# A two-layer decoder on one core: the clearings between GpSimd's indirect DMAs become a quarter as wide

## Chip, core and metric

The kernel runs on one core of one Trainium2 chip. The metric is the device time of one execution in microseconds. Engines are named as in the profile: PE is TensorE (PEld its weight loads), DVE is VectorE, ACT is ScalarE, POOL is GpSimd, SP is SyncE, which here only issues DMAs.

## What is computed

4,096 tokens of width 128 (x is 64 x 64 x 128, float32) pass six blocks. Each adds its result to its input and normalises over the 128 columns:

```python
x = _layernorm(x + _L0_attn_ref(x, ...))              # retention with xpos, group norm and gate
x = _layernorm(x + _L0_xattn_ref(ctx_2048, x, mask, mask, ...))   # masked cross-attention
x = _layernorm(x + _L0_ffn_ref(x, ...))               # 8 experts, the top 2 after rerouting by similarity
x = _layernorm(x + _L1_attn_ref(x, ...))              # 16 heads, values outside a band set to 0
x = _layernorm(x + _L1_xattn_ref(x, ctx_2048, ...))   # context joined to keys and values
x = _layernorm(x + _L1_ffn_ref(x, ...))               # encoder layer with a top-2 mixture of 8 experts
```

Two of these need rows to be moved by an index that is known only on the chip. In the third block every token picks two of its eight expert results. In the sixth every token's row goes to two experts, and two results come back.

## The kernel before

The tokens are cut into 16 groups of 256 (T = 2 tiles of 128). A group has number n * 4 + s: s is one of four slots, each with its own buffers in SBUF and two PSUM banks, and n counts four passes. The stages are:

1. First layer (about the first 477 us of the span). All eight expert results of a group are stored to a tensor y_mid of its own in HBM, and the state to x_mid.
2. Second layer (about 477 to 1375 us). For every group GpSimd fetches the two chosen expert rows of each token from y_mid by indirect DMA (`fetch`, stage "ya", L1038), and VectorE adds them up (L1583). Then come attention, cross-attention and the sixth block's own attention. At its end (stage "sc", L1102) GpSimd scatters each token's row by indirect DMA to two places in rows_x, ordered by expert.
3. Experts (1375 to about 1540 us). 39 tiles of 256 rows are loaded from rows_x, go through the expert's two matrices, and are scattered to y_rows (L1112).
4. The results are added, normalised and stored.

Every engine has one queue, and its order is written out by hand (`ORDERS`): a list of pairs (group, so many stages). `in_turn` walks through it, so instructions of four to six groups alternate on each engine, and an engine never goes past one that waits. Between engines semaphores pass (`x.of(s)`, `x.at(n, s)`). `root` (L972, L973) is the short piece of every layer norm that GpSimd does: variance plus epsilon, then the power -0.5. VectorE applies the result (L1387) and TensorE turns the normalised rows (L1829).

A fetch and a scatter are four indirect DMAs each, one for every tile t of 128 tokens and every choice k. Between two of them stands `clear_again`, three times in a fetch and three times in a scatter; the last two scatters (pass 3, slots 2 and 3) have none. It sets `blank` to zero again and, through `pool2`, makes GpSimd wait for its own instruction. `blank` is a tile of 128 x 528 float32 (4 * WIDE, where WIDE = 132 is the width of a row of rows_x). It is cleared at the start (L955) and then read by four DMAs of SyncE that fill rows_x with zeros (L844). GpSimd waits for these before the first fetch. After that nothing reads `blank`.

Other lines that the rows name: L1277, L1272 and L1625 move queries and keys out of PSUM, L1688 and L1319 spread keys and queries of the sixth block's attention, L1691 and L1630 add the bias to its values, L1065 and L1066 set parts of V and Q for the cross-attention (stage "out1"), L1059 scales attention weights.

Of the kernel before, what the change touches and what calls it, by code (L numbers as in the profile page):

```python
# [46 lines left out]
WIDE = DIM + 4  # L47
# [407 lines left out]
def build(nc, d, out, groups):  # L455
    passes = groups // SLOTS
    ctx = ExitStack()
    with ctx:
        def sb(name, shape, dt=F32):
            return ctx.enter_context(nc.sbuf_tensor(name, shape, dt))  # L460

        def sem(name):
            return ctx.enter_context(nc.semaphore(name))
# [58 lines left out]
        blank = sb("blank", [128, 4 * WIDE])  # L522
# [240 lines left out]
        dve2, pool2 = Steps(sem("dve2")), Steps(sem("pool2"))  # L763
# [190 lines left out]
        def _(pool):  # L954
# [71 lines left out]
                return pool.tensor_tensor(X1[s][:, :, :], X1[s][:, :, :], over(Row(b), T), ALU.add)  # L1026

            def clear_again():
                pool2(pool, pool.memset(blank[:, :], 0.0))

            def fetch(n, s):
                if n == 0 and s == 0:
                    pool.wait_ge(s_clear, 16 * (XROWS // 128 // BLANK))
                for t in range(T):
                    for k in range(2):
                        if t or k:
                            clear_again()
                        pool.indirect_dma_start(y_two[s][:, k, 128 * t:128 * t + 128], None, d[f"y_mid{n * SLOTS + s}"][:, :], bass.IndirectOffsetOnAxis(  # L1038
                            ap=first_rows[:, (n * SLOTS + s) * T + t, k:k + 1], axis=0)).then_inc(y_loaded[s], 16)
# [35 lines left out]
            def second2(n, s, last):  # L1075
                yield "fq.1"
                with_bias(n, s, b_x, b_x_bias, "fbo", 2)
                pool.wait_ge(b_x_ps.of(s), b_x_ps.at(n, s, use=2))
                pool.wait_ge(b_x_bias.of(s), b_x_bias.at(n, s, use=2))
                pool.tensor_tensor(X[s][:, :, :], X[s][:, :, :], over(Row("be2"), T), ALU.add).then_inc(b_x_be2.of(s), 1)  # L1080
                pool.wait_ge(b_frot.of(s), b_frot.at(n, s, 2))
                pool.tensor_tensor(qf[s], P4[s][:, 0, :], P4[s][:, 1, :], ALU.add).then_inc(b_fsum.of(s), 1)
                yield "fq.3"
                pool.wait_ge(b_frot.of(s), b_frot.at(n, s, 4))
                pool.tensor_tensor(kf[s], P4[s][:, 2, :], P4[s][:, 3, :], ALU.add).then_inc(b_fsum.of(s), 1)
                if not last:
                    yield "ya"
                    pool.wait_ge(b_s_ps.of(s), b_s_ps.at(n, s, use=5))
                    fetch(n + 1, s)
                yield "fo"  # L1090
                root(n, s, b_ln_mv, b_ln_rstd, pool2, 3)
                yield "n3"
                pool.wait_ge(b_ln_x1.of(s), b_ln_x1.at(n, s, use=0))
                scale_shift(s, "g1", "be1").then_inc(b_x1.of(s), 1)
                yield "sc"
                pool.wait_ge(b_g_done.of(s), b_g_done.at(n, s))
                pool.wait_ge(b_x1.of(s), b_x1.at(n, s))
                for t in range(T):
                    for k in range(2):
                        if (t or k) and (n < passes - 1 or s < SLOTS - 2):  # L1100
                            clear_again()
                        pool.indirect_dma_start(d["rows_x"][:, :], bass.IndirectOffsetOnAxis(  # L1102
                            ap=places[:, (n * SLOTS + s) * T + t, k:k + 1], axis=0), XW[s][:, t, :], None).then_inc(scattered[s], 16)
# [1227 lines left out]
```

## Time and profile before

| | |
|---|---|
| median of 3 runs | 1593.64 us |
| lowest and highest | 1590.29 and 1594.18 us |
| span of the profiled execution (the one time shown of it) | 1609.1 us |
| TensorE busy | 1400.8 us, 87% |
| VectorE busy | 1118.0 us, 69% |
| ScalarE busy | 933.2 us, 58% |
| GpSimd busy | 710.2 us, 44% |
| mean granted clock of TensorE | 0.953 of full speed |

The span is one execution under the profiler; the runs are timed without it. Durations and places in time below are all from that execution, in us from its start. Busy is the time in which an engine ran an instruction; issuing a plain DMA and waiting do not count. "Idle before" of an instruction is what its engine waited just before it, and the name behind the arrow is who released it.

### The profile page before, as it was taken

What the parts mean: (1) busy time and instruction counts of PE and PEld (TensorE: products, weight loads), DVE (VectorE), ACT (ScalarE), POOL (GpSimd) and SP (SyncE); (2) the same over time, 40 slices, a digit from 0 to 9 for tenths busy, and PEclk for the clock granted to TensorE, in tenths of its full rate; (3) what the DMA queues carried; (4) which work ended last, traced back from release to release, by engine and by line L of the source; (5) the groups of instructions that cost most, each with busy time, mean ns of one, the idle gap of its engine ahead of it and who ended that gap; (6) DMA issues with size and microseconds to landing.
All of it is one profiled execution on the core that took longest, in us unless ns stands there. A gap on an engine that the chain in (4) does not pass through costs nothing.

```text
span 1609.1 us, 47442 instructions
## 1 busy us (share of the span) xinstructions
PE 1400.8 (87%) x19262; PEld 1135.4 (71%) x19262; DVE 1118.0 (69%) x3476; ACT 933.2 (58%) x2469; POOL 710.2 (44%) x1048
## 2 busy tenths in 40 slices
PE   6899999999987998889989899987999985699961
PEld 4688788788765777667767677765677764588851
DVE  3777777877866657788667787677885866445456
ACT  3455556655633587754878556885568863344412
POOL 5514434434216215565244754256651343345455
PEclk8799999999998999999999999999999987799985
DMA  9942212111121001110001100011010001577761
GB/s 329 384 152 77 63 64 80 57 54 64 38 81 38 9 9 29 33 30 29 9 17 29 38 25 20 12 32 32 25 29 6 19 20 66 171 229 235 213 176 40
DMA packets 112155, 123.21 MB, mean 77 GB/s; under 512 B 21984, under 2 KB 85216, under 8 KB 111680
## 3 DMA queue, kind: packets, MB, share of 16 engines
q1 hardware_dynamic: 105344, 106.53, 21.0%
q0 software_dynamic: 6592, 13.64, 2.6%
q8 instruction: 152, 2.49, 0.7%
q14 instruction: 67, 0.55, 0.1%
HBM read 64.99 MB, written 55.15 MB: 75 GB/s over the span
## 4 chain that ended last, share of the span: by engine, by line
PE 54%; DVE 21%; ACT 9%; POOL 8%; issue 6%; another core or an unknown queue 1%; DMA 1%; SPq 0%; DVEq 0%; POOLq 0%; ACTq 0%
PE bank L1970 6%; PE bank L1837 5%; PE bank L2217 4%; PE bank L2224 4%; ACT P L1247 3%; PE bank L2092 3%; PE bank L1822 3%; PE bank L2057 3%; PE bank L1849 3%; POOL rows_x L1102 2%; PE bank L2018 2%; PE bank L2014 2%; PE bank L2007 2%; DVE P L1602 2%; PE bank L1937 2%
## 5 line engine op out<-in xcount | busy, mean ns | idle before, releaser
L1837 PE MATMUL bank<-const,P 128*128 128x128 f32 x1152 | 174.1, 283 | 14.5 <-ACT P L1247 6.1
L1837 PEld LDWEIGHTS bank<-const,P 128*128 128x128 f32 x1152 | 132.0, 144 | 48.8 <-ACT P L1247 15.5
L1247 ACT ACTIVATE P<-bank,gs 128x128 f32<-128x128 f32 x512 | 142.3, 392 | 32.2 <-DVE gs L1591 30.8
L1970 PE MATMUL bank<-XT,wb 128*128 128x256 f32 x512 | 143.2, 401 | 7.7 <-ACT PT L1152 4.3
L1059 POOL TENSOR_TENSOR P<-P,gs 128x512 f32<-128x512 f32 x64 | 66.6, 1048 | 152.5 <-DVE gs L1638 152.0
L1255 ACT ACTIVATE PT<-bank 128x512 f32<-128x512 f32 x192 | 110.5, 614 | 35.6 <-PE bank L1837 34.7
L1601 DVE TENSOR_REDUCE gs<-bank 128x8 f32<-128x512 f32 x128 | 87.3, 682 | 40.8 <-PE bank L1822 23.5
L1112 POOL DMA_INDIRECT y_rows<-R,gidx x78 | 74.7, 957 | 92.3 <-DVE R L1777 78.6
L1591 DVE TENSOR_REDUCE gs<-bank 128x4 f32<-128x512 f32 x128 | 83.0, 684 | 43.6 <-PE bank L2092 43.4
L1970 PEld LDWEIGHTS bank<-XT,wb 128*128 128x128 f32 x512 | 88.6, 193 | 25.0 <-ACT PT L1152 8.6
L972 POOL TENSOR_SCALAR rstd<-mv 128x2 f32<-128x2 f32 x80 | 17.9, 224 | 195.1 <-DVE mv L1379 194.2
L1348 ACT ACTIVATE PT<-bank,Q 128x256 f32<-128x256 f32 x156 | 64.6, 475 | 56.7 <-PE bank L2217 49.3
L1240 ACT ACTIVATE P<-P 128x512 f32<-128x512 f32 x128 | 81.5, 644 | 24.2 <-DVE P L1602 22.1
L1219 ACT ACTIVATE P<-bank 128x256 f32<-128x256 f32 x128 | 48.5, 380 | 77.6 <-PE bank L1970 76.9
L1602 DVE TENSOR_TENSOR P<-bank,gs 128x512 f32<-128x512 f32 x128 | 88.5, 692 | 4.4
L2217 PE MATMUL bank<-XT,Q 128*128 128x256 f32 x312 | 86.1, 388 | 2.9 <-ACT XT L1344 2.7
L2224 PEld LDWEIGHTS bank<-Q,PT 128*128 128x128 f32 x624 | 79.5, 192 | 7.0 <-issue 3.3
L1102 POOL DMA_INDIRECT rows_x<-XW,places x64 | 64.4, 1006 | 44.8 <-DVE places L1728 28.9
L1849 PE MATMUL bank<-wb,P 128*128 128x128 f32 x512 | 79.5, 280 | 4.5 <-DVE P L1532 4.2
L2224 PE MATMUL bank<-Q,PT 128*128 128x128 f32 x624 | 81.2, 276 | 1.9 <-issue 1.8
L1849 PEld LDWEIGHTS bank<-wb,P 128*128 128x128 f32 x512 | 72.5, 192 | 14.1 <-DVE P L1532 9.7
L1038 POOL DMA_INDIRECT Q<-y_mid,first_rows x64 | 63.4, 990 | 31.8 <-DVE first_rows L1577 16.1
(298 smaller groups left out, 3815.0 us busy)
## 6 DMA issues: line engine op xcount, KB each, us to landing
Q<-in_wm SPq DMA_DIRECT2D x39, 578.5 KB
rows_x<-blank SPq DMA_DIRECT2D x4, 5016.0 KB, 37.8
y_mid<-PT SPq DMA_DIRECT2D x16, 512.0 KB, 2.9
y_mid<-D SPq DMA_DIRECT2D x16, 512.0 KB, 2.9
XW<-rows_x SPq DMA_DIRECT2D x39, 132.0 KB
wb<-in_wb SPq DMA_DIRECT2D x1, 4228.0 KB, 15.5
V<-in_ctxT SPq DMA_DIRECT2D x32, 128.0 KB, 2.7
XT<-in_xT SPq DMA_DIRECT2D x16, 128.0 KB, 2.2
```

The lines of the kernel that those rows point to most:

```text
L1102: pool.indirect_dma_start(d["rows_x"][:, :], bass.IndirectOffsetOnAxis(ap=places[:, (n * SLOTS + s) * T + t, k:k + 1], axis=0), XW[s][:, t ...
L1240: act.activation(P[s][:, i, :], P[s][:, i, :], ACT.Exp, scale=scale).then_inc(p.of(s), 1)
L1247: ins = act.activation(P[s][:, i, 128 * g:128 * g + 128], banks[s][i][:, 128 * g:128 * g + 128], ACT.Exp, bias=gs[s][:, 0, 4 * i + g:4 * i ...
L1255: act.activation(dst[:, i, :], banks[s][i][:, :], ACT.Copy).then_inc(pT.of(s), 1)
L1591: dve.tensor_reduce(gs[s][:, 0, 4 * i:4 * i + 4], banks[s][i][:, :].rearrange("p (g m) -> p g m", m=128), AX.X, ALU.min).then_inc(b_s_sub. ...
L1601: st2(dve.tensor_reduce(mx, v, AX.X, most))
L1602: dve.tensor_tensor(P[s][:, i, :].rearrange("p (g m) -> p g m", m=width), v, each(mx, width), ALU.subtract).then_inc(s_sub.of(s), 1)
L1837: last = pe.transpose(tile(banks[s][i], t), tile(P[s][:, i, :], t), ident)
L1849: last = mm(tile(half(s, i + 1), t), tile(P4[s][:, i + 1, :], t), tile(B("down"), e), start=True, stop=True)
L1970: mm(half(s, 2 * (e % 2) + k), tile(B("gu"), 2 * e + k), XT[s][:, :], start=True, stop=True).then_inc(a_up_ps.of(s), 1)
L2217: mm(half(s, c), tile(part(wm[s], WM, "w1"), c), XT[s][:, :], start=True, stop=True).then_inc(m_up_ps.of(s), 1)
L2224: ins = mm(tile(half(s, 0), t), tile(PT4[s][:, c, :], t), tile(part(wm[s], WM, "w2"), c), start=c == 0, stop=c == NC - 1)
```

## The change

The 90 later clearings write columns 0 to 131 of `blank` and not all 528. The first clearing, which the DMAs read, stays as wide as it was.

```diff
             def clear_again():
-                pool2(pool, pool.memset(blank[:, :], 0.0))
+                pool2(pool, pool.memset(blank[:, 0:WIDE], 0.0))
```

## Rows read from the trace of the kernel before

**Rows 1.** The page's head: busy us, share of the span, instructions.
```profile
span 1609.1 us, 47442 instructions
PE 1400.8 (87%) x19262; PEld 1135.4 (71%) x19262; DVE 1118.0 (69%) x3476; ACT 933.2 (58%) x2469; POOL 710.2 (44%) x1048
```

**Rows 2.** The page: the chain that ended last, by engine.
```profile
PE 54%; DVE 21%; ACT 9%; POOL 8%; issue 6%; another core or an unknown queue 1%; DMA 1%; SPq 0%; DVEq 0%; POOLq 0%; ACTq 0%
```

**Rows 3.** Groups of GpSimd: shapes, count, busy us, mean ns, idle before.
```profile
L1029 POOL MEMSET blank<- 128x528 f32 x90 | 50.0, 555 | 0.2
...
L1066 POOL MEMSET V<- 128x256 f32 x16 | 5.0, 311 | 0.0
...
L964 POOL MEMSET Q<- 128x16 f32 x4 | 0.3, 125 | 0.1
```

**Rows 4.** Timeline of GpSimd in one scatter: start, us, instruction, idle before.
```profile
667.18 1.09 POOL L1102 DMA_INDIRECT rows_x<-XW,places  x1 [0.43 <-DVE places L1728]
668.28 0.56 POOL L1029 MEMSET blank<- 128x528 f32 x1
669.12 1.00 POOL L1102 DMA_INDIRECT rows_x<-XW,places  x1 [0.28 <-POOL blank L1029]
670.11 0.56 POOL L1029 MEMSET blank<- 128x528 f32 x1
670.95 0.97 POOL L1102 DMA_INDIRECT rows_x<-XW,places  x1 [0.28 <-POOL blank L1029]
```

**Rows 5.** The chain in order of time: first and last of 33 clearings.
```profile
477.55 0.57 POOL blank L1029
...
1311.08 0.55 POOL blank L1029
```

**Rows 6.** Timeline of GpSimd in the last two scatters.
```profile
1364.39 0.96 POOL L1102 DMA_INDIRECT rows_x<-XW,places  x1 [0.30 <-issue]
1365.66 0.96 POOL L1102 DMA_INDIRECT rows_x<-XW,places  x1 [0.31 <-issue]
```

**Rows 7.** Timeline of TensorE where the chain returns from GpSimd, directly or not.
```profile
491.26 0.69 PE L1829 MATMUL bank<-const,X 128*128 128x128 f32 x2 [7.94 <-DVE X L1387]
...
502.73 0.46 PE L2030 MATMUL bank<-K,Q 64*64 64x64 f32 x16 [0.57 <-DVE V L1630]
...
679.84 1.10 PE L1822 MATMUL bank<-D,Q 64*64 64x128 f32 x32 [1.61 <-DVE V L1691]
...
700.90 0.44 PE L1829 MATMUL bank<-const,X 128*128 128x128 f32 x2 [1.63 <-DVE X L1387]
...
740.19 0.44 PE L1829 MATMUL bank<-const,X 128*128 128x128 f32 x2 [0.44 <-DVE X L1387]
...
893.06 1.81 PE L1822 MATMUL bank<-D,Q 64*64 64x128 f32 x32 [1.46 <-ACT Q L1319]
...
952.17 0.44 PE L1829 MATMUL bank<-const,X 128*128 128x128 f32 x2 [0.17 <-DVE X L1387]
...
972.53 0.44 PE L1829 MATMUL bank<-const,X 128*128 128x128 f32 x2 [1.21 <-DVE X L1387]
...
1164.29 0.66 PE L1837 MATMUL bank<-const,P 128*128 128x128 f32 x4 [1.09 <-POOL P L1059]
...
1314.64 0.69 PE L1829 MATMUL bank<-const,X 128*128 128x128 f32 x2 [0.76 <-DVE X L1387]
```

**Rows 8.** Timeline of other engines at those places.
```profile
677.76 1.60 DVE L1688 TENSOR_SCALAR D<-K,const 128x256 f32<-128x256 f32 x2 [0.64 <-POOL K L1085]
...
698.84 0.60 DVE L1387 TENSOR_SCALAR X<-R,mv,rstd 128x128 f32<-128x128 f32 x2 [1.28 <-POOL rstd L973]
...
891.25 1.70 ACT L1319 ACTIVATE Q<-K,const 128x256 f32<-128x256 f32 x4 [0.81 <-POOL K L1082]
...
970.90 1.56 DVE L1387 TENSOR_SCALAR X<-R,mv,rstd 128x128 f32<-128x128 f32 x2 [0.42 <-POOL rstd L973]
...
1308.31 0.97 POOL L1102 DMA_INDIRECT rows_x<-XW,places  x1 [1.50 <-issue]
```

**Rows 9.** Stretches: us, busy us and count by engine, granted clock, DMA share, GB/s.
```profile
684.00:691.00 7.00, 7.00 (x154) 6.24 (x152) 5.79 (x29) 3.66 (x9) 3.19 (x4) 0.68 0.12 32
1313.00:1320.00 7.00, 6.03 (x31) 4.83 (x31) 2.87 (x8) 1.15 (x3) 5.36 (x9) 0.51 0.08 23
```

## The prediction

> **What bounds the kernel now.** I read the page's head first, then the chain of work that ended last, then GpSimd's groups, and last the timeline around each clearing that stands on the chain. The head shows TensorE busy in 87% of the span and GpSimd in 44% [rows 1]. The chain gives TensorE 54% of the span, VectorE 21%, ScalarE 9% and GpSimd 8% [rows 2]. The kernel is therefore bound by TensorE and by the hand-overs to it, and GpSimd matters only where its queue is the last thing that others wait for. That happens around the indirect DMAs: GpSimd runs its stages in a fixed order, so the small root (L972, L973) that a layer norm waits for stands behind four indirect DMAs and three clearings.
>
> The groups show 90 clearings of 128x528 at 555 ns, 50.0 us together [rows 3]. The timeline of one scatter shows the beat: indirect DMA 1.09, clearing 0.56, 0.28 of hand-over, next DMA [rows 4]. I then went through the chain in eighteen stretches of 90 us and counted: 33 of the 90 clearings are on it, the first at 477.55 and the last at 1311.08 [rows 5]. The other 57 lie beside longer work.
>
> **The change part by part.** Only the width of the memset changes. No instruction, DMA, wait or place in a queue is added, removed or moved. blank is read only by the four DMAs at the start, and nothing reads what the later clearings write.
>
> What a 128x132 memset takes is not in the trace, so I bound it. A 128x16 memset takes 125 ns and a 128x256 one 311 ns [rows 3]; these are the ends. Between them the slope is 186/240 = 0.775 ns a column, which gives 125 + 116 x 0.775 = 215 ns. Between 256 and 528 columns the slope is 244/272 = 0.90, which gives 311 - 124 x 0.90 = 200 ns. I take 208. A clearing then gives back 555 - 208 = 347 ns (244 to 430 at the ends). Ninety of them free 31.2 us of GpSimd. A group of three, which is one fetch or one scatter, gives 1.04 us. The 33 on the chain give 33 x 0.347 = 11.5 us at most.
>
> Could the indirect DMA refuse to come sooner, so that a wait replaces the clearing? In the last scatters, which have no clearings, the next one starts 0.30 us after the end of the one before and still takes 0.96 us [rows 6]: a beat of 1.26 us. The new beat would be 0.96 + 0.21 + 0.28 = 1.45 us, slower than that, so nothing of the kind stands in the way.
>
> How much of the 11.5 us arrives? GpSimd comes earlier by up to 1.04 us a group; an engine can use of that only what it had been idle just before, since its own queue is late next. The ten places where a stretch of the chain with clearings returns to the others [rows 7, 8]:
>
> - 491.26, behind two fetches (six clearings): TensorE had been idle 7.94 us. All of 6 x 0.347 = 2.08 counts.
> - 502.73, behind the third fetch: idle 0.57. 0.57.
> - 679.84, behind a scatter: TensorE idle 1.61, but VectorE's D (L1688), which hands over to it, had been idle only 0.64. 0.64.
> - 700.90: idle 1.63. 1.04.
> - 740.19: idle 0.44. 0.44.
> - 893.06: TensorE idle 1.46, but it waits for ScalarE's Q (L1319), and that one had been idle 0.81. 0.81.
> - 952.17: idle 0.17. 0.17.
> - 972.53: TensorE idle 1.21, but VectorE's X (L1387) only 0.42. 0.42.
> - 1164.29: idle 1.09. 1.04.
> - 1314.64: idle 0.76. One of the three clearings there is followed by 1.50 us in which GpSimd waited for nothing shown [rows 8]; I take it that this gap stays and swallows its share, and count two: 0.69.
>
> The sum is 7.90 us, 69% of 11.5. That is after one meeting with other queues. Behind each place come further ones, where another slot's work is late next. I have no row that adds these up; I take the same share once more, 7.90 x 0.69 = 5.4 us. The 57 clearings off the chain I cost at nothing. Their cover is TensorE's work of other slots, and the relief only keeps their groups from becoming late when the rest moves up by 5 us. If the cover went, they would be worth at most 57 x 0.347 = 19.8 us, which I see no sign of: TensorE's idle time outside those ten places is spread over other releasers.
>
> The port between VectorE and GpSimd: VectorE's pair of normalisations (L1387) takes 0.60 us at 698.84, and 1.56 us at 970.90, where GpSimd runs memsets of V and Q alongside (the stage "out1", L1065 and L1066) [rows 8]. So a memset of GpSimd can hold up a VectorE operation of this form. The Trainium skill, page SBUF — State Buffer, section "Who interferes with whom", states that VectorE in a two-port mode and GpSimd exclude each other for a whole instruction; by it this pair is what rows 8 show, and shorter clearings would hold VectorE for less. The rule has a side that speaks against the change as well: an indirect DMA that comes sooner takes the port sooner. Out of rows, GpSimd's instructions fill (0.96 + 0.56)/1.79 = 85% of a beat before and (0.96 + 0.21)/1.45 = 81% after, so the balance is slightly in favour, and I cost it at nothing.
>
> The sum is made on the profiled execution (span 1609.1 us, the one time of it that is shown); the median of the runs is 15.5 us below. A difference of 5.4 us carries over: 1593.6 - 5.4 = 1588.2 us, -0.34%.
>
> **The rivals.**
>
> *A. Hidden (no change).* GpSimd's relief is taken up by the other queues a few microseconds later. For: TensorE is busy 87% of the span, and at three returns (740.19, 952.17, 972.53) an idle time of 0.44 us or less caps the gain [rows 7, 8]. Against: the opening at 491.26 is a plain stall of 7.94 us with nothing else to do, and it alone gives 2.1 us. If only that and a third of the remaining 5.8 us arrive, the time is 1593.6 - 4.0 = 1589.6; if only that, 1591.6. Both are within 0.3% (4.8 us), which is about what a measurement of this kernel can tell from no change.
>
> *B. All of it, and clock on top.* Every clearing on the chain pays, 11.5 us: 1582.1. Right behind two of the returns TensorE's granted clock is down: 0.68 over 684 to 691 and 0.51 over 1313 to 1320, that is at 1.2 instead of 2.4 GHz for two thirds or nearly all of the time, each after idle time of TensorE [rows 9]. If a smaller stall there no longer brings the clock down, 6.03 us of matmuls at 0.51 become 6.03 x 0.51 = 3.1 us, another 2.9 us each. One such stretch beside 7.9 us of relief gives 1582.8.
>
> *C. Slower: the clock the other way.* The same mechanism with the opposite sign. Places where TensorE now keeps 2.4 GHz see its idle time fall elsewhere when GpSimd's hand-overs come earlier than the partner's, and gain low stretches. One stretch like that of 1313 to 1320 costs 2.9 us. It decides the sign from the second (5.8 against 5.4 us), and four net (11.6 - 5.4 = +6.2, 1599.8) make it slower by over 0.3%. For: low stretches come after stalls of 1 to 2 us, and there are many places near that. Against: order and work of every engine stay as they were, every release comes no later than before, and idle time of TensorE shrinks on the whole.
>
> *D. The change does not do what it says,* because a memset has a floor near the old price: excluded by the 125 and 311 ns rows [rows 3].
>
> **How the numbers follow.** The forecast (4.8 to 9 us less) gets 0.45, B (9 us or more less) 0.09, A (within 4.8 us of before) 0.40, C 0.06. So faster by over 0.3% is 0.54, within 0.3% 0.40, slower by over 0.3% 0.06. The predicted time is 1588.2. Downwards the range ends at 1581.5, just past the full 11.5 us; upwards at 1594.5, which takes in A whole and a low stretch of the clock that eats the 2.1 us of the opening.
>
> **What would show it right or wrong.** In the profile of the changed kernel: L1029 still 90 times, near 208 ns; GpSimd's busy time down by 31 us to 679; the beat inside a fetch at 1.45 us with the indirect DMAs still at 0.95 to 0.97; the stall at 491.26 down from 7.94 to about 5.9 us; the ten returns earlier by the amounts above, within their caps. TensorE's busy time should stay within the few microseconds that its clock moves. The prediction is wrong if the indirect DMAs grow longer when they follow each other sooner, if the 0.28 us of hand-over grows by what the clearing lost, or if low stretches of the clock come or go in number: that is the largest term I cannot size, some 3 us each.

## The result and the profile after

The changed kernel takes 1572.22 us (median of 4 runs, 1568.92 to 1576.02); the kernel before took 1593.91 us in the same session (1590.29 to 1598.14). The ratio is 0.9868 with a 95% interval of 0.9843 to 0.9894: 21 us or 1.3% faster, between 17 and 25 us. The forecast was 1588.2 us, 5.4 us faster, with a range down to 1581.5. The sign was right and the size was a quarter of the real one.

The profiled execution of before that the prediction rests on was a long one: 1609.1 us of span [rows 1], while the run of the second profile below took 1594.15 us for a span of 1592.3. The kernel before was therefore profiled once more (experiment 1). Where not said otherwise, "before" is now that second profile. The head of the page and the chain by engine, first of before, second profile:

```profile
span 1592.3 us, 47442 instructions
PE 1394.5 (88%) x19262; PEld 1133.8 (71%) x19262; DVE 1117.1 (70%) x3476; ACT 935.3 (59%) x2469; POOL 710.2 (45%) x1048
...
PE 52%; DVE 22%; POOL 10%; ACT 9%; issue 6%; DMA 1%; SPq 0%; DVEq 0%; POOLq 0%; ACTq 0%
```

and of the changed kernel:

```profile
span 1569.1 us, 47442 instructions
PE 1385.0 (88%) x19262; PEld 1124.8 (72%) x19262; DVE 1114.3 (71%) x3476; ACT 934.2 (60%) x2469; POOL 680.4 (43%) x1048
...
PE 54%; DVE 21%; ACT 9%; POOL 8%; issue 5%; DMA 1%; SPq 0%; DVEq 0%; POOLq 0%; ACTq 0%
```

GpSimd is busy 29.8 us less. TensorE, with the same 19,262 matmuls, is busy 9.5 us less (15.8 less than in the first profile of before, whose 1400.8 us show how far two executions differ); the forecast put that at nothing. The groups of GpSimd in the changed kernel:

```profile
L1102 POOL DMA_INDIRECT rows_x<-XW,places x64 | 64.4, 1006 | 44.5 <-DVE places L1728 29.4 <-POOL blank L1029 11.4 <-issue 3.7
L1038 POOL DMA_INDIRECT Q<-y_mid,first_rows x64 | 63.4, 990 | 31.8 <-DVE first_rows L1577 16.1 <-POOL blank L1029 13.0 <-issue 2.7
...
L1029 POOL MEMSET blank<- 128x132 f32 x90 | 20.3, 226 | 0.2
```

A clearing takes 226 ns and not 555 [rows 3], so each gives back 329 ns and all ninety 29.7 us. The indirect DMAs take what they took. The same scatter as in [rows 4], in the changed kernel:

```profile
659.31 1.09 POOL L1102 DMA_INDIRECT rows_x<-XW,places  x1 [0.43 <-DVE places L1728]
660.41 0.23 POOL L1029 MEMSET blank<- 128x132 f32 x1
660.92 0.97 POOL L1102 DMA_INDIRECT rows_x<-XW,places  x1 [0.28 <-POOL blank L1029]
661.88 0.23 POOL L1029 MEMSET blank<- 128x132 f32 x1
662.39 0.97 POOL L1102 DMA_INDIRECT rows_x<-XW,places  x1 [0.28 <-POOL blank L1029]
```

The beat is 1.47 us and was 1.8; the hand-over of 0.28 us is untouched.

**Where the time went.** The first indirect DMA starts at 473.0 us in both traces, so the first layer gave nothing. From the last scatter's last DMA to the end it is 1592.3 - 1361.5 = 230.8 us and 1569.1 - 1339.1 = 230.0. All but 0.8 us of the difference lies between, in the second layer. I cut it at the first DMA of the scatters number 1, 4, 5, 8, 9 and 12, which gives three stretches with scatters and two long pieces between them. A stretch holds three scatters and two fetches, 15 clearings; the long piece behind it holds the fourth scatter and two fetches, 9 clearings, with some 80 us without any between them. The columns are us, busy us and count of TensorE, its weight loads, VectorE, ScalarE and GpSimd, then TensorE's granted clock. Before:

```profile
662.25:747.53 85.28, 74.31 (x1158) 57.77 (x1159) 69.68 (x217) 45.00 (x113) 53.27 (x72) 0.94 0.10 30
747.53:877.28 129.75, 121.80 (x2191) 94.29 (x2189) 92.04 (x226) 102.13 (x278) 52.50 (x80) 0.99 0.08 21
877.28:956.51 79.23, 71.15 (x1155) 55.50 (x1156) 66.89 (x216) 44.53 (x111) 53.52 (x72) 0.98 0.11 32
956.51:1086.58 130.07, 119.61 (x2190) 92.71 (x2190) 92.67 (x225) 101.68 (x277) 52.47 (x81) 1.00 0.08 21
1086.58:1169.44 82.86, 72.76 (x1153) 56.76 (x1151) 66.70 (x214) 43.83 (x109) 52.99 (x72) 0.96 0.11 31
```

Changed:

```profile
659.31:738.01 78.70, 70.42 (x1158) 54.30 (x1159) 69.40 (x217) 44.67 (x113) 48.30 (x73) 1.00 0.11 33
738.01:867.97 129.96, 121.12 (x2191) 94.07 (x2189) 92.00 (x226) 101.98 (x277) 49.52 (x80) 0.99 0.08 21
867.97:944.38 76.41, 69.47 (x1157) 53.96 (x1156) 67.03 (x216) 44.56 (x112) 48.54 (x72) 1.00 0.11 34
944.38:1072.38 128.00, 119.68 (x2190) 92.73 (x2190) 91.47 (x225) 101.67 (x277) 49.72 (x80) 1.00 0.08 21
1072.38:1149.53 77.15, 70.15 (x1153) 53.66 (x1151) 65.88 (x214) 43.62 (x109) 48.03 (x72) 1.00 0.11 33
```

Up to the first scatter the changed kernel gains 662.25 - 659.31 = 2.9 us, all of it at the opening. The three stretches with scatters gain 6.6, 2.8 and 5.7 us, the two long pieces -0.2 and 2.1, and the rest, from scatter 12 to the last one's last DMA, 2.5 (192.1 and 189.6 us). The 15 clearings of a stretch are 4.9 us of relief, so two of the three gain more than their clearings give back. TensorE's busy time falls in them by 3.9, 1.7 and 2.6 us, and its granted clock rises from 0.94, 0.98 and 0.96 to 1.00.

How finely may one pair of profiles be read? The first indirect DMA, with the same work before it, starts between 473.0 and 477.6 us in the profiles of experiments 1 to 9 and 12; that two of them agree at 473.0 is luck. Four profiles have the clearings of before: its own two and those of experiments 10 and 11. In them the three stretches take 83.6 to 85.3, 79.2 to 80.8 and 79.8 to 84.0 us, so a single stretch differs by up to 4 us from one execution to the next. The means of the four lie 5.8, 3.4 and 4.7 us above the changed kernel, 13.9 us together for 14.8 us of relief. The clock does go with the clearings: of the twelve stretches only one, in experiment 10, has it at 1.00, and all three do in the changed kernel. That one:

```profile
1086.58:1166.34 79.76, 70.16 (x1152) 53.62 (x1151) 66.54 (x214) 43.73 (x109) 53.04 (x72) 1.00 0.11 32
```

### The profile page after: what moved, and what is told of

It is laid out like the page before. It is cut to its first block, busy times and chain, and to the rows that moved or that the text cites. A ratio compares the mean times of both kernels' runs of the same rounds, so it can differ in the third digit from the quotient of the medians.

```text
span 1569.1 us, 47442 instructions
## 1 busy us (share of the span) xinstructions
PE 1385.0 (88%) x19262; PEld 1124.8 (72%) x19262; DVE 1114.3 (71%) x3476; ACT 934.2 (60%) x2469; POOL 680.4 (43%) x1048
## 4 chain that ended last, share of the span: by engine, by line
PE 54%; DVE 21%; ACT 9%; POOL 8%; issue 5%; DMA 1%; SPq 0%; DVEq 0%; POOLq 0%; ACTq 0%
PE bank L1970 6%; PE bank L1837 5%; PE bank L2217 4%; PE bank L2224 4%; ACT P L1247 3%; PE bank L2057 3%; PE bank L2092 3%; PE bank L1849 3%; PE bank L2018 3%; POOL rows_x L1102 2%; PE bank L2007 2%; PE bank L1822 2%; PE bank L2014 2%; DVE P L1602 2%; DVE gs L1601 2%
## 5 line engine op out<-in xcount | busy, mean ns | idle before, releaser
L1240 ACT ACTIVATE P<-P 128x512 f32<-128x512 f32 x128 | 82.1, 647 | 24.9 <-DVE P L1602 24.3
L1038 POOL DMA_INDIRECT Q<-y_mid,first_rows x64 | 63.4, 990 | 31.8 <-DVE first_rows L1577 16.1
## 6 DMA issues: line engine op xcount, KB each, us to landing
wb<-in_wb SPq DMA_DIRECT2D x1, 4228.0 KB, 15.1
```

The source lines that it names most:

```text
L1240: act.activation(P[s][:, i, :], P[s][:, i, :], ACT.Exp, scale=scale).then_inc(p.of(s), 1)
```

## The experiments

Each kernel was timed in five rounds beside the kernel before; times in us are medians, intervals belong to the ratio.

**1. The kernel before again.** No edit.

> The kernel before, once more, for a second profile. The profiled execution of before had a span of 1609.1 us, 15 us above the runs, while that of the changed kernel (1569.1) lies 2 us below its runs. Theory N (the first profile was a slow draw, its extra low stretches of TensorE's clock are not the kernel's own): the span here is 1588 to 1598 and the low stretches between 477 and 1337 us add up to under 40 us. Theory K (the low stretches are tied to the stalls behind the indirect DMAs, at every execution): the same seven low stretches in that part, about 44 us. Time in both: same as before, ratio 1.00.

Measured: 1594.15 against 1593.53 (1.0007, 0.9989 to 1.0024), span 1592.3. Theory N is right that the first profile had been a long draw, and wrong about the clock: between 477 and 1337 us the two profiles have 44.4 and 44.6 us at the lower level, as theory K said, though not at the same places. The chain, counted in pieces of 40 us, holds 45 of the 90 clearings here and not 33: the nine of the opening again, and 12 scatters where the first profile had 8. The four scatters that are new begin at 899, 1087, 1108 and 1169 us. No fetch behind the opening is on either chain. The first clearing on the chain, one of each new scatter, and the last:

```profile
474.24 0.57 POOL blank L1029
...
899.89 0.57 POOL blank L1029
...
1087.68 0.56 POOL blank L1029
...
1108.71 0.57 POOL blank L1029
...
1170.53 0.57 POOL blank L1029
...
1303.52 0.55 POOL blank L1029
```

**2. No clearings.**

```diff
-                pool2(pool, pool.memset(blank[:, :], 0.0))
+                pass
```

> No clearing at all between the indirect DMAs, so the beat falls from 1.79 to about 1.26 us (against 1.45 with 132 columns). The clearings after the first are left out; nothing reads them. Theory P (GpSimd's time is worth nearly a constant share wherever it is taken away: 21.7 us for 29.7 us of clearing, 0.73): GpSimd gets back 90 x 0.53 = 48 us, and the time falls by about 35 us, to 1559. Theory Q (the gain of 132 columns came from a shorter hold on the port that VectorE shares, so that removing the beat's free 0.28 us works the other way): the time is at or above that of the changed kernel, 1572 or more. Theory R (by the caps of the prediction, the gain runs out): about 1568, little below the changed kernel.

Measured: 1569.76 (0.9844, 0.9830 to 0.9857), 24.9 us faster. From 132 columns to none GpSimd gets back 18 us more and the time falls by about 4 us, less than the two intervals can tell apart. The gain runs out, as theory R had it, and theory P's 35 us is refuted. Theory Q (no faster than the changed kernel) is not: the difference is too small for that, and experiment 9 has to decide.

**3 and 4. Only the fetches, only the scatters narrow** (`clear_again` gets a width, WIDE in one of its two calls).

> 132 columns only in the 48 clearings of the fetches, 528 in the 42 of the scatters. Theory P: 48/90 of the gain, 11.6 us, ratio 0.993. Theory S (only the scatters count, since seven of the ten places on the chain are behind scatters; the fetches give the opening stall alone): 2 to 3 us, ratio 0.998.

> 132 columns only in the 42 clearings of the scatters. Theory P: 42/90 of the gain, 10.1 us, ratio 0.994. Theory S: 18 to 19 us, ratio 0.988. If both halves together with e3 make clearly less than 21.7 us, the two kinds cover for each other; if more, each alone already frees what the other would.

Measured: fetches 1589.07 (0.9969, 0.9958 to 0.9981), 4.9 us for 15.8 us of relief; scatters 1579.19 (0.9909, 0.9894 to 0.9924), 14.5 us for 13.8 us of relief. Together 19.4, near the whole. The expectation of equal shares is refuted by both. Theory S had 2 to 3 us for the fetches, the near edge of what was measured (3.0 to 6.7), and 18 to 19 for the scatters, above what was measured (12 to 17). A scatter's clearings are worth about all of their time. A fetch's are worth a third on average, but the nine of the opening alone give 3 us, as the timeline further down shows, so that the 39 others are left with some 2 us for 12.8 us of relief.

**5. Two short clearings for one.**

```diff
-                pool2(pool, pool.memset(blank[:, :], 0.0))
+                pool2(pool, pool.memset(blank[:, 0:24], 0.0))
+                pool2(pool, pool.memset(blank[:, 0:24], 0.0))
```

> Each clearing becomes two of 128x24, each waited for: about 2 x (0.13 + 0.28) = 0.82 us between indirect DMAs, nearly the 0.83 of the kernel before, but GpSimd's memsets fill only 0.27 us of it and not 0.56. Theory P (GpSimd's time in its queue is what counts): as before, ratio 0.998 to 1.002. Theory Q (the hold on the port that VectorE shares is what counts): most of the 21 us gain comes, ratio 0.990 or less. In between: the share that the port has.

Measured: 1577.51 (0.9899, 0.9878 to 0.9921). The expectation had a wrong term: the second memset follows the first after 0.07 us, not 0.28, so the gap between DMAs (from the end of one to the start of the next) was 0.60 us and not 0.82. The kernel does not separate the theories; it is one more point on the line of gaps. In its trace:

```profile
661.89 1.09 POOL L1103 DMA_INDIRECT rows_x<-XW,places  x1 [0.43 <-DVE places L1729]
662.99 0.14 POOL L1029 MEMSET blank<- 128x24 f32 x1
663.19 0.12 POOL L1030 MEMSET blank<- 128x24 f32 x1
663.59 1.06 POOL L1103 DMA_INDIRECT rows_x<-XW,places  x1 [0.28 <-POOL blank L1030]
```

**6. Every clearing twice** (the memset of 528 columns stands there two times).

> Each clearing of 128x528 is made twice: 50 us more of GpSimd's time, beat 2.6 us or so with its second hand-over. Theory P (nearly every clearing lies on the path through the stretches with scatters, 0.65 us of time per us of GpSimd): at least 0.83 x 90 x 0.65 = 48 us slower. Theory R (caps: only the places on the chain, as the prediction had it, 33 to 45 of 90): 0.83 x 33 to 0.83 x 45 = 27 to 37 us slower.

Measured: 1645.26 (1.0323, 1.0300 to 1.0345), 51.5 us slower; gap 1.44 us, so 55 us more of GpSimd's time. Upwards 0.94 of every microsecond arrives. Theory R, by which only the clearings of the two chains count, is refuted: it allowed 37 us. Of the caps this run says nothing, since idle time before an instruction limits what it can gain and not what it can lose. In its trace:

```profile
672.75 0.56 POOL L1029 MEMSET blank<- 128x528 f32 x1
673.36 0.54 POOL L1030 MEMSET blank<- 128x528 f32 x1
674.18 0.98 POOL L1103 DMA_INDIRECT rows_x<-XW,places  x1 [0.28 <-POOL blank L1030]
```

**7 and 8. Narrow only where the first profile's chain had clearings (33), and only elsewhere (57).** A counter picks the groups:

```diff
+            NARROW = {"fetch": (0, 1, 2), "sc": (0, 1, 2, 4, 6, 7, 10, 12)}
...
+                width = WIDE if kinds[kind] in NARROW[kind] else 4 * WIDE
+                pool2(pool, pool.memset(blank[:, 0:width], 0.0))
```

> 132 columns only in the 33 clearings that the chain of the first profile holds (the first three fetches; the scatters number 1, 2, 3, 5, 7, 8, 11 and 13 in the order of the queue), 528 in the other 57. The prediction's bookkeeping: these alone carry the gain, 5.4 to 7.9 us, and the other 57 nothing, so this kernel would be as fast as the whole change. Theory P (the rest of the groups are late by next to nothing and count as well): 33/90 of 21.7 = 8 us here, and the remaining 13 to 14 us in the other kernel.

> The complement: 132 columns only in the 57 clearings that the chain of the first profile does not hold. The prediction's bookkeeping: 0 us, ratio 1.000. Theory P: 57/90 of 21.7 = 13 to 14 us faster, ratio 0.991. If the two kernels together give much less than 21.7 us, the gain needs both, because each group's relief is swallowed where the next group is still long.

Measured: on the chain 1580.46 (0.9920, 0.9902 to 0.9938), 12.8 us (10 to 16) for 10.9 us of relief; off it 1588.23 (0.9967, 0.9955 to 0.9979), 5.3 us (3 to 7) for 18.8 us. Together 18, not clearly less than 21. So the clearings on the first chain carry their relief fully (1.2 us a us), not at 0.47, and the rest is not free (0.28).

That the first chain picked the right clearings does not follow. Its 33 are the nine of the opening and 24 of scatters; the other 57 are 39 of fetches and 18 of scatters. By experiment 4 a scatter's clearing is worth 14.5 / 42 = 0.345 us. If each has that worth, on the chain or off it, the first kernel gains 3.0 + 24 x 0.345 = 11.2 us, which is inside what was measured, and the second 18 x 0.345 = 6.2, with about 2 us for the fetches 8. If a scatter off the first chain is worth nothing, the second has those 2 us alone. The measured 5.3 lies between. The chain of the second profile comes nearest: it adds four of the six scatters, 12 x 0.329 = 3.9 us, and with the fetches that makes 6. The runs do not separate the three.

**9. Time without memory.** One clearing of 24 columns and twelve empty instructions.

```diff
-                pool2(pool, pool.memset(blank[:, :], 0.0))
+                pool2(pool, pool.memset(blank[:, 0:24], 0.0))
+                for _ in range(12):
+                    apart(pool)
```

> Between indirect DMAs one clearing of 128x24 and twelve empty instructions, which touch no memory, in place of the clearing of 128x528. What the empty ones take isn't known; the trace gives the gap g from the end of one indirect DMA to the start of the next. The kernels so far give for gaps of 1.44, 0.83, 0.60, 0.50 and 0.30 us the times +51, 0, -16.8, -21.4 and -24.8 us. Theory P (only time in GpSimd's queue counts): the time at this gap lies on that line. Theory Q (what counts is the hold on VectorE's port): at a gap near 0.83 the time is still 10 us or more under the line, since GpSimd's memsets fill 0.13 us of the gap and not 0.56.

Measured: 1601.98 (1.0051, 1.0035 to 1.0068), 8.1 us slower. Its trace:

```profile
668.48 0.14 POOL L1029 MEMSET blank<- 128x24 f32 x1
669.41 0.99 POOL L1104 DMA_INDIRECT rows_x<-XW,places  x1 [0.79 <-POOL blank L1029]
670.39 0.14 POOL L1029 MEMSET blank<- 128x24 f32 x1
671.31 0.96 POOL L1104 DMA_INDIRECT rows_x<-XW,places  x1 [0.78 <-POOL blank L1029]
```

The gap is 0.92 us, 0.09 more than before; 90 x 0.09 = 8.1 us, and the line through gaps 0.83 and 1.44 gives 0.09 x 51.5/0.61 = 7.6 us. The memset fills 0.14 us of the gap and not 0.56, and nothing of a gain is seen. That refutes the port as the carrier; the interval, 5.6 to 10.8 us slower, leaves room for a part of some 2 us. VectorE's pair of normalisations (L1387 before, L1389 here) does get shorter, from 468 to 427 ns on average in this kernel, and in the changed kernel to 406. That is the direction that the rule of the Trainium skill (SBUF — State Buffer, "Who interferes with whom") asks for; it is only not what the time hangs on. The group before, and in this kernel:

```profile
L1387 DVE TENSOR_SCALAR X<-R,mv,rstd 128x128 f32<-128x128 f32 x96 | 37.4, 468 | 22.1 <-POOL rstd L973 21.9
```

```profile
L1389 DVE TENSOR_SCALAR X<-R,mv,rstd 128x128 f32<-128x128 f32 x96 | 35.4, 427 | 26.4 <-POOL rstd L973 26.2
```

**10. TensorE kept busy in the opening stall** (26 transposes of the identity ahead of the first wait, behind two waits that keep their PSUM bank free).

```diff
                 yield "t1"
+                if n == 0 and s == 0:
...
+                    for k in range(26):
+                        pe.transpose(tile(banks[s][0], k % T), ident, ident)
                 pe.wait_ge(b_x.of(s), b_x.at(n, s, use=0))
```

> The kernel before, clearings of 528, with 26 more transposes of the identity on TensorE in the stall at the start of the second layer (idle for about 8 us up to 491); they write a PSUM bank that is overwritten right after. GpSimd's work is as before. Theory C (the low stretch of TensorE's clock, 10 us, follows from that stall and costs time of its own): the low stretch there goes or shrinks, and the time falls by 2 to 4 us. Theory P alone (the path waits for GpSimd there anyway): no change within 0.1%, or slower by what the transposes overrun the stall.

Measured: 1594.97 (1.0005, 0.9993 to 1.0018). The granted clock in the 27 us from the first fetch rose from 0.73 to 0.84 (first before, then here), and the time did not move:

```profile
473.00:500.00 27.00, 17.57 (x74) 12.36 (x73) 12.37 (x40) 6.82 (x17) 23.03 (x31) 0.73 0.25 74
```

```profile
474.70:501.70 27.00, 19.42 (x98) 14.31 (x97) 12.37 (x40) 6.80 (x17) 23.03 (x31) 0.84 0.23 68
```

The forecast of 2 to 4 us is refuted at this place.

**11. The same at the 15 other groups, four transposes each**, again behind waits that keep the bank free.

```diff
                 yield "t1"
...
+                if n or s:
+                    for k in range(4):
+                        pe.transpose(tile(banks[s][0], k % T), ident, ident)
                 pe.wait_ge(b_x.of(s), b_x.at(n, s, use=0))
```

> The kernel before with four more transposes (about 1.1 us of TensorE) ahead of the wait for the normalised state at the start of each other group's second layer, 15 places, so that some of TensorE's stalls of 0.4 to 1.6 us are filled. Theory C (a good part of the 21 us is TensorE's clock, which falls after such stalls): low stretches between 600 and 1337 us fall from 31 to 34 us to under 15, and the time is lower in spite of 16 us more of matmuls, by 1 to 5 us. Theory P alone: slower, by up to 16 us, where the stall is shorter than the filling.

Measured: 1595.24 (1.0012, 1.0002 to 1.0022). The clock was not held up: 0.98 between 603 and 1333 us as before, and 0.955 as the median of the runs of both kernels. So it says nothing for or against the clock. What it does show: TensorE was busy 1404.9 us and not 1394.5, 10.4 us more, and the time grew by 2 us. TensorE's own work is mostly not what ends last at these places.

**12. 264 columns.**

```diff
-                pool2(pool, pool.memset(blank[:, :], 0.0))
+                pool2(pool, pool.memset(blank[:, 0:2 * WIDE], 0.0))
```

> Clearings of 128x264, about 0.33 us, gap 0.60, as in the kernel with two of 128x24. Theory P: the same time as that kernel, 1577 us, ratio 0.990, though GpSimd's memsets fill 0.33 us of the gap and there 0.26. Theory Q (port): slower than that kernel, by its part of the hold: 1581 or more.

Measured: 1580.35 (0.9921, 0.9906 to 0.9937), gap 0.62 us. By the ratios it is 3.5 us above experiment 5, of which 90 x 0.02 = 1.8 us is the gap; the intervals overlap, and no part for the port can be read from it.

All kernels with equal gaps, time as the ratio makes it of 1594 us:

| between indirect DMAs | gap us | GpSimd's time | time | share that arrives |
|---|---|---|---|---|
| 528 columns twice | 1.44 | +55 | +51.5 | 0.94 |
| 24 columns, empty instructions | 0.92 | +8 | +8.1 | 1.0 |
| 528 columns (before) | 0.83 | 0 | 0 | |
| 264 columns | 0.62 | -19 | -12.6 | 0.67 |
| 24 columns twice | 0.60 | -21 | -16.1 | 0.78 |
| 132 columns (the change) | 0.50 | -29.7 | -21.0 | 0.71 |
| nothing | 0.30 | -48 | -24.9 | 0.52 |

The quickest median is that with nothing, 1569.76 us, but its interval and that of the change overlap.

## Why the prediction was wrong

It was right in the direction, in the prices, and in what the clearings are: time in GpSimd's queue. What failed is how much of that time arrives: it let the 33 clearings on the chain count for 5.4 us and the 57 others for nothing, and by themselves they measured 12.8 and 5.3 us.

- **The price of a memset.** 208 ns taken, 226 measured, inside the ends of 125 and 311. The relief is 29.7 and not 31.2 us; that error points the other way.
- **The beat.** 1.45 us forecast, 1.47 measured, DMAs and hand-over unchanged. "Nothing of the kind stands in the way" held.
- **The opening.** Forecast: the stall falls by 2.08 us. Before 6.47 us, changed 4.50, a fall of 1.97 = 6 x 0.329. The timeline of TensorE, first before, then changed:

```profile
487.95 0.69 PE L1829 MATMUL bank<-const,X 128*128 128x128 f32 x2 [6.47 <-DVE X L1387]
...
499.42 0.46 PE L2030 MATMUL bank<-K,Q 64*64 64x64 f32 x16 [0.45 <-DVE V L1630]
```

```profile
485.97 0.69 PE L1829 MATMUL bank<-const,X 128*128 128x128 f32 x2 [4.50 <-DVE X L1387]
...
496.45 0.46 PE L2030 MATMUL bank<-K,Q 64*64 64x64 f32 x16
```

- **The caps.** The next place failed at once. The prediction capped the third fetch at 0.57 us, TensorE's idle time before L2030. Before, L2030 started at 499.42; changed, at 496.45 with no idle time ahead of it. That is 2.97 us for nine clearings (9 x 0.329 = 2.96), so the third fetch brought its full 0.99. A cap by the idle time just before holds only if the engine's own queue stands still, and it had moved as well, since what it did before waited for earlier results of GpSimd.
- **"I take the same share once more."** This step had no row. It turned 7.9 us into 5.4, after the caps had turned 11.5 into 7.9. Experiment 7 measured the same 33 clearings by themselves: 12.8 us (10 to 16), all of their 10.9 us of relief. So neither discount was there, the 3.6 us of the caps as little as these 2.5. That the work behind a release moves up on all engines together is shown at the opening and argued for the rest.
- **"The 57 clearings off the chain I cost at nothing."** Experiment 8: 5.3 us (3 to 7). The second profile of the same kernel puts 45 clearings on its chain, so which groups are on it changes from one execution to the next. The 12 that it adds are all among these 57 and come to 3.9 us. What the near-critical scatters bring was a missing term; the fetches behind the opening are worth little indeed.
- **"At most 11.5 us."** This bound came from one chain and from durations that stay. With 45 clearings it is 45 x 0.329 = 14.8 us, still under the 17 of the interval's near end. What goes beyond needs other instructions on the chain that get shorter. Two kinds did: TensorE's matmuls where the clock is up, and L1387.
- **TensorE's clock, costed at nothing.** TensorE is busy 9.5 us less over the span, and in the stretches with scatters the clock goes to 1.00. Rival B had it as a gain on top, but sized it at one stretch of 2.9 us (by its own rule the stretch from 684 gives 7.00 x 0.32 = 2.2, not 2.9) and gave the whole case 0.09.

How much of the 21 us is the clock is not shown by an experiment. As bookkeeping, the three stretches with scatters are 15.1 us shorter, 8.2 of it less busy and 6.9 less idle time of TensorE. That is no proof of cause: less busy time counts only where TensorE ends last, and experiment 10 raised the clock of one stretch without a gain, while experiment 11 failed to raise it. Experiments 7 and 8 say which clearings bring the gain, the clock's part included; they do not split it. A kernel that holds TensorE's clock up through all stalls and changes nothing else would, and none was found.

The timed runs give an estimate. Over the 68 runs of the kernel before, with mean clocks from 0.946 to 0.961, 0.001 more of clock goes with 0.39 us less of time (0.2 to 0.6), or with 0.26 if the slowest run is left out. From 0.955 to 0.962, the medians before and after, that makes 2 to 3 us, at most 4 or so, a small part of the 21. It supposes that what goes together between the runs of one kernel does so for the change as well.

Rival A (hidden) and rival C (slower by the clock) are refuted, the latter with its sign: fewer stalls, higher clock. The caps are refuted at the third fetch and by experiment 7. The table's falling share (0.94, 0.71, 0.52) does show that the gain runs out, only later than the caps had it.

## What to carry to other kernels

An engine that is busy 44% of the time was worth 0.7 to 0.94 us of time per us of its work here, because its queue is fixed and others wait behind it in bursts; ask what its queue costs inside the burst, not over the span. Do not multiply the local gains of a chain by a loss that no row shows: here the clearings on the chain paid in full, and groups just off the chain counted too, so their relief was nearer to a lower end than to an upper one. Two profiles of the same kernel show how far the chain can be trusted: here one had 33 of 90 clearings on it and the other 45, and the kind of place that was on neither, the fetches behind the opening, was the kind that brought little. Profiles of the same kernel also say how finely a pair may be read: a stretch of 80 us differed by up to 4. And try the other direction once, since the doubled clearing gave the price of GpSimd's time more plainly than any reading.

## What was not expected of the hardware

- Two memsets of GpSimd in a row, the second behind a wait for the semaphore of the first, are 0.06 to 0.07 us apart; a memset and an indirect DMA are 0.28 us apart, whatever the width (experiments 5 and 6).
- Twelve empty instructions of GpSimd cost about 0.78 - 0.28 = 0.5 us, 0.04 each (experiment 9).
- TensorE's mean granted clock followed the gaps. The medians of the timed runs are 0.943 with doubled clearings, 0.955 before, 0.959 with 264 columns, 0.962 with 132 and 0.961 with none. Ten more microseconds of matmuls, spread over the waits in small portions, did not raise it (0.955, experiment 11); 26 transposes in the one long stall raised it a little (0.958, experiment 10) and the time stayed.
